# Local attention of a two-layer decoder: VectorE splits the output before its second rotation in step 2, and copies weights ahead of the maxima in step 3

## What is computed

```python
q = (h @ Wq.T) ...; k = (h @ Wk.T) ...; v = (h @ Wv.T) ...      # 16 query heads, 4 key/value heads, 128 wide
q = rms_norm(q, qn_w); k = rms_norm(k, kn_w)
q = q * cos + rotate_half(q) * sin; k = k * cos + rotate_half(k) * sin
scores = einsum('bhgtd,bhkd->bhgtk', q * 128**-0.5, k)          # group g: 4 query heads that share a key head
scores = where(0 <= distance <= 64, scores, lowest)
att = softmax(scores); ctx = einsum('bhgtk,bhkd->bhgtd', att, v)
out = ctx @ Wo.T
```

## Time and profile before

| | us |
|---|---|
| three runs | 1516.11, 1518.3, 1518.98; median 1518.3 |
| the profiled execution, its own time | 1528.93 |
| its span in the profile | 1526.9 |
| mean granted TensorE clock | 0.923 of full speed |
| stretch of the local attention | about 675 to 1176 us of the span |

### The profile page before, as it was taken

One profiled execution on the slowest core, in us unless ns is written; L12 is line 12 of the kernel. 1 busy time (PEld: TensorE's weight loads), 2 busy tenths in 40 slices (PEclk: granted clock), 3 DMA queues, 4 the chain that ended last, 5 costly groups with the idle time before them and its releaser, 6 DMA issues. The chain is left out here.

```text
span 1526.9 us, 26479 instructions
## 1 busy us (share of the span) xinstructions
PE 1277.1 (84%) x7839; PEld 998.6 (65%) x7886; DVE 986.3 (65%) x1905; ACT 850.0 (56%) x2174; POOL 643.4 (42%) x724
## 2 busy tenths in 40 slices
PE   6994998886875998648989998999887888878998
PEld 5672555546664886536777777777775555657887
DVE  5997888872633534797777777777774566653443
ACT  5452999983242545456666666666653465552332
POOL 2003666654353024367666666666664323310000
PEclk9997999996896999959999999999999899998999
DMA  8401333300012453020000000000000000000000
GB/s 313 143 0 41 84 83 100 92 15 0 0 63 89 150 201 106 28 100 0 2 1 0 0 0 0 0 0 0 0 1 3 5 3 3 3 0 1 15 14 28
DMA packets 49684, 64.52 MB, mean 42 GB/s; under 512 B 6032, under 2 KB 42896, under 8 KB 48336
## 3 DMA queue, kind: packets, MB, share of 16 engines
q1 hardware_dynamic: 46544, 55.27, 11.5%
q0 software_dynamic: 3072, 8.39, 1.6%
HBM read 38.48 MB, written 16.78 MB: 36 GB/s over the span
## 5 line engine op out<-in xcount | busy, mean ns | idle before, releaser
L2209 ACT ACTIVATE wi_weights<-wi_psum,wi_bias,wi_scale 128x128 f32<-128x128 f32 x256 | 114.5, 457 | 115.0 <-DVE wi_bias L2319 115.0
L929 ACT ACTIVATE gq_weights<-gq_psum,gq_least 128x128 f32<-128x128 f32 x512 | 152.0, 525 | 2.0 <-DVE gq_least L977 2.0
L1984 POOL TENSOR_TENSOR wi_straight<-wi_straight,wi_crossed 128x512 f32<-128x512 f32 x80 | 109.7, 1372 | 5.8 <-DVE wi_crossed L2305 5.7
L977 DVE TENSOR_REDUCE gq_least<-gq_psum 128x4 f32<-128x512 f32 x128 | 86.2, 687 | 26.6 <-PE gq_psum L854 25.9
L1972 POOL TENSOR_TENSOR wi_scratch<-wi_sums,wi_eps 128x4 f32<-128x4 f32 x80 | 36.1, 451 | 158.6 <-DVE wi_sums L2288 157.3
L2310 DVE TENSOR_REDUCE wi_top<-wi_psum 128x4 f32<-128x512 f32 x64 | 44.0, 688 | 72.8 <-PE wi_psum L2099 72.8
L1973 POOL TENSOR_TENSOR wi_scale<-wi_scratch,minus_half 128x4 f32<-128x4 f32 x80 | 84.6, 1058 | 6.3
L2121 PE MATMUL wi_psum<-wi_wo_high,wi_out_high 128*128 128x256 f32 x256 | 47.5, 309 | 41.5 <-DVE wi_out_low L2273 38.8
L862 PE MATMUL gq_psum<-const,gq_weights 128*128 128x128 f32 x512 | 78.5, 276 | 1.3 <-ACT gq_weights_t L937 0.4
L2305 DVE TENSOR_TENSOR wi_crossed<-wi_raw,wi_sin_q 128x256 f32<-128x256 f32 x128 | 78.8, 655 | 0.0
L2108 PE MATMUL wi_psum<-wi_weights_t,wi_values 128*128 128x512 f32 x128 | 76.3, 681 | 0.8 <-DVE wi_weights_t L2326 0.8
(11 more groups left out here) (384 smaller groups left out, 3931.3 us busy)
## 6 DMA issues: line engine op xcount, KB each, us to landing
gq_keys<-in_ctx_keys_dram SPq DMA_DIRECT2D x16, 512.0 KB, 3.8
gq_keys_diagonal<-gq_key_parts SPq DMA_DIRECT2D x64, 128.0 KB, 3.9
slot_x<-rw_zero SPq DMA_DIRECT2D x1, 5120.0 KB, 17.9
ex_slot_rows<-slot_x SPq DMA_DIRECT2D x20, 256.0 KB, 3.0
slot_y<-ex_s_out SPq DMA_DIRECT2D x20, 256.0 KB, 2.1
x<-in_x_dram SPq DMA_DIRECT2D x4, 512.0 KB, 8.5
gate<-in_gate_dram SPq DMA_DIRECT2D x2, 1024.0 KB, 5.7
up<-in_up_dram SPq DMA_DIRECT2D x2, 1024.0 KB, 7.9
```

Of the source, the lines that this page charges most:

```text
L929: e = act.activation(weights[:, u % RINGS, j * P:j * P + P], ps[:, u % 4, j * P:j * P + P], ACT.Exp, bias=least[:, u % 4, j:j + 1], scale= ...
L977: dve.tensor_reduce(least[:, u % 4, :], rows(u), AX.X, ALU.min).then_inc(topped, 1)
L1984: added_up = pool.tensor_tensor(straight[:, at], straight[:, at], crossed[:, at], ALU.add)
L2209: act.activation(weights[:, g % 2, j, :], ps[:, SC + g % 2, j * P:j * P + P], ACT.Exp, bias=bias[:, g % 2, j:j + 1], scale=scale[:, g, j:j ...
```

## The change

Two edits in DVE's stream of the local attention. `split_out` (and `finish`, which only runs in step 1, where there is no second rotation) now stands ahead of the second rotation. That alters the order in step 2 alone, where the second rotation is not empty. And in step 3 the copy of group 2's transposed weights, `take_weights(t, 2)`, stands ahead of `maximum(t, 3)` instead of behind it. No instruction is added or removed, on any engine; the other engines' streams are as before.

```diff
                 for g in range(U):
                     if g == 0 and not last:
                         normalise(t + 1, 1 - s)
+                    if g == 3:
+                        take_weights(t, 2)
                     maximum(t, g)
-                    if g > 0 or not first:
+                    if g < 3 and (g > 0 or not first):
                         pt, _, pg = earlier(t, s, g, 1, U)
                         take_weights(pt, pg)
                     shift(t, g)
@@
                     for item in items[:1]:
                         rotate(*item)
                     invert(t, g)
-                    for item in items[1:]:
-                        rotate(*item)
                     if g == 1 and not first:
                         finish(t - 1)
                     if g > 0 or not first:
                         pt, _, pg = earlier(t, s, g, 1, U)
                         split_out(pt, pg)
+                    for item in items[1:]:
+                        rotate(*item)
                     if g == 0 and not last:
                         split_h(t + 1, 1 - s)
```

## The result

The changed kernel takes 1493.95 us (median of 4 runs, 1491.88 to 1494.55) against 1518.48 for the kernel before (4 runs, 1516.11 to 1518.98): 24.5 us less. The ratio is 0.9839, 95% interval 0.9822 to 0.9856. In microseconds the interval is a saving of 21.9 to 27.0. A second measurement of the same kernel, later, gave 1493.24 against 1516.89, ratio 0.9842 (0.9823 to 0.9860). The forecast was 1491, from 1486 to 1506, with 1491 from case A.

The account below looks back on a forecast made before the run. TensorE, busy 84%, was taken as the bound, its clock falling behind a wait for DVE. 14 x 1.97 + 0.37 = 27.9 us, less 0.7 in the last batch, gave 27 saved: 1518.3 - 27 = 1491, range 1486 to 1506.

Parts of the forecast that it names:

- case A: Local attention: the summed forecast holds, 27 us saved, 1491 us, own range 1486 to 1497; chance 0.66.
- The list of waits: PE's product with Wo waits for DVE's low part 15 times, 38.8 us, once in every batch but the last.
- PE's wait for the low part hides a clock: Behind PE's 2.66 us wait the clock falls; 1.60 of 1.97 us saved per batch is clock.
- The low part is there before PE asks, and the copy of the weights is late next: Split first: low part ready at 859.05, the 2.66 us wait goes; PE's gap before attend becomes 1.4 us.
- The rotation ends 0.18 us later, not 0.89: DVE's rotation of q0, taking turns with POOL, ends at 862.78, 0.18 us later, though it starts 0.89 later.
- the other reading: Each instruction keeps its length: q0's rotation stays 4.52 us, ends 863.49; 16.6 us saved, 1502 us; chance 0.14.
- Bias, exponentials, copy of q0: ACT's chain before the next scores: shift about 864.02, exponentials 864.20, copy of q0 starts 2.72 us later, ends 867.54.
- The score product 0.3 us after that copy's end: Next batch's score product on PE comes at 867.82, 0.3 us for hand-over and mask's matmul; frame 7.74 us.
- No fall of the clock with a gap of 1.4 us: PE's longest gap becomes 1.4 us; granted clock stays near 1.00, as in the stage's tail windows.
- case C: Clock still falls once per batch, or fell less often in runs without a profile: 1501 to 1515 us; chance 0.12.
- Edit 2: Step 3, copy of weights ahead of maxima: copy ends 863.38, attend starts 863.52, PE's gap 1.4 us instead of 2.66.
- The last batch loses by the copy ahead of the maxima: Last batch, step 3: maxima wait for the copy, at most its 0.68 us, so 0.7 us lost.

Follow-up runs that it names:

- f1: Kernel before, order unchanged, with PE repeating the four transposes of group 2's weights six times more in step 3 of every batch but the last: 1495.51 us.
- l1: Changed kernel without POOL's product of k with its scale (L1987), so it computes something else: 1477.89 us.
- e1: Kernel before with only the split moved ahead of q0's rotation, the copy of the weights staying behind the maxima: 1501.87 us.
- e3: e1 with PE's transposes of group 2's weights repeated four times more in step 3: 1491.76 us.
- e2: Kernel before with only the copy of group 2's weights moved ahead of the maxima: 1519.15 us.

## Why the prediction was right

Case A came in, with 24.5 us where the sum had 27.3, and for the reasons given. Point by point:

- **The list of waits**: its 15 entries are not one in every batch but the last, as I read them. They are 14 of 2.66 to 2.69 us and one of 1.5 us at the end of the stage; the 2.65 us of the first batch are booked under another name, `issue`. The count of 15 long gaps was right all the same, by luck.
- **PE's wait for the low part hides a clock**: right, and f1 shows it by itself. In the sum, 1.60 of the 1.97 us per batch were clock; filling the gap, with no change of order, gave 21.6 us, where 14 x 1.60 is 22.4.
- **The low part is there before PE asks, and the copy of the weights is late next**: right. The split starts 1.70 us before the transposes (839.56), the gap ahead of `attend` is 1.31 us, forecast 1.4.
- **The rotation ends 0.18 us later, not 0.89**: right. The sin products end at 843.95, 2.69 us after the transposes; forecast 2.70 (862.78 - 860.08), and 3.41 by the other reading. The rotation's length is 3.78 us, forecast 3.8, and 4.52 by the other reading. POOL's L1987 ends 0.90 us after the cos product (843.34, 842.44); the sum had 0.84. The rule of the Trainium skill's page "SBUF — State Buffer", in "SBUF: two separate sides", stands on the side of the reading that held, and the traces agree with it for POOL's instructions on 128x512 (the ends 0.54 to 0.56 us behind POOL's, above). For POOL's L1973 on 128x4 they do not: there DVE's second sin product begins and ends within L1973's row, though by the rule it would wait for L1973's end. POOL's rows are rough, but the two products took 0.76 us there and 0.75 with POOL idle (l1), so for these the measurement decides against the rule.
- **Bias, exponentials, copy of q0**: forecast 3.94, 4.12 and 6.84 us after the transposes; measured 3.92, 4.12 and 6.83.
- **The score product 0.3 us after that copy's end**: this is the term that was mis-sized. From the end of ACT's copy (848.09 + 0.62 = 848.71) to the product (849.19) it is 0.48 us, so that the frame is 7.93 and not 7.74 us. 0.19 x 15 = 2.9 us, which is about the distance between 27.3 and the 24.5 measured; the run times alone, with their 21.9 to 27.0, could hardly tell, but the period of 28.80 us against 28.6 forecast says the same. The second profile of the changed kernel shows how the 0.48 divides. There the copy ends at 847.81 and the mask's matmul has its record: 0.25 us of hand-over, and 0.22 from the mask to the product.

```profile
847.19 0.62 ACT L2200 ACTIVATE wi_q_t<-wi_psum 128x512 f32<-128x512 f32 x1
```

```profile
848.06 0.39 PE L2096 MATMUL wi_psum<-wi_mask,wi_ident 128*128 128x512 bf16 x1 [0.97 <-ACT wi_q_t L2200]
848.28 1.05 PE L2099 MATMUL wi_psum<-wi_k_t,wi_q_t 128*128 128x128 f32 x8
```

- **No fall of the clock with a gap of 1.4 us**: right, 1.00 from 720 to 1120 us in both profiles of the changed kernel. The margin was smaller than I thought: at 1.9 us (e1) the clock falls in 10 batches of 15. Had the copy stayed behind the maxima, case C would have come, and I had written nothing that tells 1.4 from 1.9: the tail's window that I leaned on had one gap of 1.97 us and no fall, but one gap is a small sample. That part of the forecast was in part luck.
- **Edit 2**: I had put its worth into an earlier `attend` without saying that ACT hides it. e1's batch with the clock up has the frame of the changed kernel, and e3 its time. Its worth is the 0.6 us by which the gap is shorter.
- **The last batch loses by the copy ahead of the maxima**: the wait for normalise there is 2.5 us. In the stage of the kernel before, PE's longest idle for the same cause was 2.0; so about 0.5, of the 0.7 put down. Against the first scores of the batch the bias of step 3 comes 0.53 us later. Between e2, which has it without a gain, and the kernel before it is within the noise.

The count over the stage agrees. PE's transposes of k and q0 start 14 periods apart at 714.22 and 1142.55 us before, at 701.50 and 1104.65 after: 30.60 us each against 28.80, 25.2 us over the 14. The stretch from the first maxima to the last differs by 22.3 us only, for two reasons outside these 14 periods. Ahead of them the profile after is 1.5 us longer, with a mean granted clock of 0.82 there (672.56 to 701.50 us) against 0.94 before (686.76 to 714.22). Behind them it is 1.4 us longer, because the last maxima now stand behind the copy and the last scores wait for ACT.

## What to carry to other kernels

Price an idle gap of TensorE by what the clock does behind it, not by its length: compare the same piece of work behind a gap with the granted clock at 1.00 and below, and if they differ, a shorter gap, or even useless matmuls in it, may be worth more than the wait itself. Where DVE and POOL both work on large operands in SBUF (128x256 and 128x512 here), lay the sum out instruction by instruction, whoever is ready first going first, and put DVE's work on PSUM beside POOL's instructions. After each step ask again what is late next: here it was in turn the low part, the copy and the bias, POOL's scaling of k, and POOL's normalise.

## What the runs showed that I had not expected

The fall of the clock depends on fractions of a microsecond of standstill once per batch of 29 to 31 us: behind 2.66 us it fell in 14 batches of 15, behind 1.9 in 10 of 15, behind 1.3 never between 720 and 1120 us. I know no reason from these runs for which of the gaps of 1.9 us it falls behind. And 24 repeated matmuls in every batch but the last, in a kernel whose TensorE is the busiest engine, made it 21.6 us faster.
